# Attention row sums: half of the keys summed by ScalarE in PSUM, the other half as one chained slab

## The reference

```
h   = gamma * layernorm(x) + beta            # gamma, beta from the condition vector
qkv = h @ Wqkv.T + bqkv                       # split into q, k, v of 16 heads, 32 channels each
att = softmax(q @ k.T) / sqrt(512)            # per head, 1024 x 1024
out = (att @ v) @ Wp.T + bp
h1  = out + x
y   = gamma * layernorm(h1) + beta + h1
```

## Time and profile before

| | us |
|---|---|
| median of three runs (lowest, highest) | 1467.18 (1466.33, 1473.64) |
| the profiled execution | 1469.42 |
| its span, first to last instruction | 1467.8 |
| PE busy in the span | 1376.5 (94%) |
| POOL busy | 1004.2 (68%) |
| DVE busy | 918.7 (63%) |
| ACT busy | 708.4 (48%) |

### The profile page before, as it was taken

The page is one execution under the profiler, slowest core; times in us unless marked ns, Lnnn a source line. Parts: engine busy times, 40 slices in busy tenths (PEclk is TensorE's granted clock), DMA queues, the critical chain, the costliest instruction groups (busy, mean ns, idle before and its releaser), DMA issues.

```text
span 1467.8 us, 35271 instructions
## 1 busy us (share of the span) xinstructions
PE 1376.5 (94%) x10884; PEld 906.9 (62%) x10884; DVE 918.7 (63%) x1634; ACT 708.4 (48%) x1371; POOL 1004.2 (68%) x763
## 2 busy tenths in 40 slices
PE   6898999999999999999999999999999989898994
PEld 4888666656565767666666767666555545544562
DVE  5345766666666666666666666666666666666525
ACT  4121455555555545555454545555454545454441
POOL 2443455656565778688786978776898777778935
PEclk9899999999999999999999999999999999999997
DMA  7567533333434444455354444435453323332221
GB/s 232 149 185 224 130 97 100 100 98 102 114 101 115 118 121 137 117 139 141 108 144 122 135 110 136 116 113 141 116 134 85 103 85 102 86 101 87 76 60 61
DMA packets 216697, 174.01 MB, mean 119 GB/s; under 512 B 105492, under 2 KB 186516, under 8 KB 216632
## 3 DMA queue, kind: packets, MB, share of 16 engines
q1 hardware_dynamic: 214456, 166.83, 42.4%
q0 software_dynamic: 1984, 6.29, 1.2%
q10 hardware_dynamic: 192, 0.07, 0.0%
HBM read 113.29 MB, written 58.51 MB: 117 GB/s over the span
## 4 chain that ended last, share of the span: by engine, by line
PE 60%; POOL 18%; issue 12%; POOLq 3%; DVE 3%; DMA 1%; ACT 1%; SPq 1%; DVEq 0%; ACTq 0%
PE ps_a L744 12%; PE ps_st L758 10%; PE ps_o L775 10%; POOL p L1509 9%; PE ps_w L709 7%; PE ps_w L656 7%; PE ps_s L788 6%; PE ps_st L709 3%; POOLq L1369 2%; DVE half_max L1237 1%; POOL y_t L1426 1%; POOL y_t L1424 1%; PE ps_w L822 1%; POOL oT_s L1400 1%; PE ps_s L709 1%
## 5 line engine op out<-in xcount | busy, mean ns | idle before, releaser
L1237 DVE TENSOR_REDUCE half_max<-ps_a 128x1 f32<-128x512 f32 x1024 | 670.1, 687 | 404.1 <-PE ps_a L744 403.6
L1013 ACT ACTIVATE p<-ps_st 128x512 f32<-128x512 f32 x1024 | 565.9, 597 | 458.8 <-PE ps_st L758 427.5
L1509 POOL TENSOR_TENSOR p<-p 128x1024 f32<-128x1024 f32 x248 | 591.0, 2386 | 265.9 <-PE ps_o L775 264.3
L744 PE MATMUL ps_a<-k_stack,q_stack 96*128 96x512 f32 x1024 | 449.7, 441 | 14.7 <-DVE half_max L1237 10.7
L758 PE MATMUL ps_st<-q_stack,k_stack 98*128 98x512 f32 x1024 | 409.8, 402 | 15.2 <-ACT p L1013 14.6
L744 PEld LDWEIGHTS ps_a<-k_stack,q_stack 96*128 96x128 f32 x1024 | 194.0, 190 | 186.3 <-issue 94.8
L775 PE MATMUL ps_o<-p,v_head 128*32 128x256 f32 x4096 | 273.4, 385 | 0.0
L758 PEld LDWEIGHTS ps_st<-q_stack,k_stack 98*128 98x128 f32 x1024 | 196.4, 192 | 49.2 <-ACT p L1013 28.2
L775 PEld LDWEIGHTS ps_o<-p,v_head 128*32 128x32 f32 x4096 | 134.5, 111 | 91.3 <-issue 5.3
L788 PE MATMUL ps_s<-p,root_s 128*32 128x256 f32 x1984 | 160.5, 395 | 11.1 <-POOL p L1509 9.7
L709 PEld LDWEIGHTS ps_w<-hT_s,wqkv_s 128*128 128x128 f32 x1056 | 144.3, 189 | 11.0
(11 more groups left out here) (167 smaller groups left out, 1004.3 us busy)
## 6 DMA issues: line engine op xcount, KB each, us to landing
qk_scratch<-qkT_s SPq DMA_DIRECT2D x108, 256.0 KB, 2.4
q_stack<-qk_scratch SPq DMA_DIRECT2D x192, 128.0 KB, 2.8
k_stack<-qk_scratch SPq DMA_DIRECT2D x192, 128.0 KB, 3.0
x_tile<-in_x SPq DMA_DIRECT2D x34, 256.0 KB, 5.0
gq_s<-gain_bias_scratch SPq DMA_DIRECT2D x16, 512.0 KB, 4.4
v_scratch<-v_parts SPq DMA_DIRECT2D x32, 256.0 KB, 3.3
v_head<-v_scratch SPq DMA_DIRECT2D x64, 128.0 KB, 2.1
att_scratch<-o_stage SPq DMA_DIRECT2D x240, 32.0 KB, 1.5
```

Source lines behind the costliest of these rows:

```text
L744: pe.matmul(ps_a[:, parity, :], q_stack[0:96, s, t * 128:(t + 1) * 128], k_stack[0:96, s, half * 512:(half + 1) * 512], start=True, stop=T ...
L1013: nc.scalar.activation(p32[:, k, e * 512:(e + 1) * 512], ps_st[:, ST_BANK[2 * k + e], :], ACT.Exp).then_inc(exp_done, 1)
L1237: V.tensor_reduce(half_max[:, s % 2, item:item + 1], ps_a[:, parity, :], AX.X, ALU.max).then_inc(a_used, 1)
L1509: G.tensor_tensor(p32[:, 2 * j + 1, :], p32[:, 2 * j, :], p32[:, 2 * j + 1, :], ALU.add).then_inc(pair_added, 1)
```

## The change

Row sums are made in another way, and the maxima with them:

- A slab's two score matmuls (queries on partitions) now go to two neighbouring banks of a three-bank `ps_a`: the keys 512 to 1023 into bank 0 or 2 in turn (the kept bank), the keys 0 to 511 always into bank 1 (the shared bank). One DVE reduction over both banks (1024 columns) gives the negated maximum at once. `half_max` and its join are gone.
- ACT then takes the exponential of the kept bank in place, with `neg_max` as bias and an accumulator, which gives each query's sum over half of the keys (`slab_sum`, into `col_sums`). That is one more ACT operation of 512 columns in each step, beside the two it has.
- The other half of the keys is slabs 0 to 3 of the turned exponentials. POOL adds 0 to 1, that to 2, that to 3: three chained adds instead of four separate ones (`slab_add`).
- PE's row sums come once a head, in step 1 of the next (`row_sums`): 16 matmuls of 128 columns, 8 with `root_s` on slab 3 and 8 that turn `col_sums` with a scaled identity. They go into the free half of `ps_o`; `ps_s` is gone, its bank went to `ps_a`.
- ACT copies all 512 columns of `ps_o` in one instruction and waits for the row sums too. In the last iteration DVE's `end_norm` reads that copy.
- The turn of the maxima into a row uses the shared bank, after the slab of step 4. The start of the program puts 12 slabs where it had 25 items, and its projections use other banks.

The core of the diff:

```diff
-PAIR_ADD_STEP = {0: 2, 2: 3, 4: 0, 6: 1}
+SLAB_ADD_STEP = {4: 0, 6: 1, 7: 2}
...
-        ps_a = ctx.enter_context(nc.psum_tensor("ps_a", [128, 2, 512], F32))
+        ps_a = ctx.enter_context(nc.psum_tensor("ps_a", [128, 3, 512], F32))
         ps_o = ctx.enter_context(nc.psum_tensor("ps_o", [128, 512], F32))
-        ps_s = ctx.enter_context(nc.psum_tensor("ps_s", [128, 512], F32))
...
+        def slab_banks(t):
+            return (0, 1) if t % 2 == 0 else (2, 1)
...
+            def a_half(g, s, t, half, slab, uses):
+
+                kept, shared = slab_banks(t)
+                if half:
+                    need(pe, a_summed, slab - 1)
...
+                else:
+                    need(pe, a_used, uses)
+                mm = pe.matmul(ps_a[:, kept if half else shared, :], q_stack[0:96, s, t * 128:(t + 1) * 128],
+                               k_stack[0:96, s, half * 512:(half + 1) * 512], start=True, stop=True)
...
+            def turn(s, uses):
+
+                pe.wait_ge(a_used, uses)
+                pe.transpose(ps_a[0:8, 1, 0:128], neg_max[:, s % 2, :], f_ident).then_inc(a_ready, 1)
...
-            def pair_sums(g, s, j):
+            def row_sums(g, s):
...
+                pe.wait_ge(slab_added, 3 * v + 3)
+                pe.wait_ge(a_summed, 8 * v + 8)
+                for h in range(2):
+                    cols = slice(QW + h * 128, QW + h * 128 + 128)
+                    for e in range(4):
+                        pe.matmul(ps_o[HD * e:HD * e + HD, cols], root_s[:], p32[:, 3, e * QW + h * 128:e * QW + h * 128 + 128],
+                                  start=True, stop=False)
+                    for e in range(4):
+                        mm = pe.matmul(ps_o[HD * e:HD * e + HD, cols], col_sums[:, s, 2 * e + h:2 * e + h + 1].to_broadcast([128, HD]),
+                                       root_ident[:], start=False, stop=True)
...
                 act.wait_ge(pv_done, 4 * v + 4)
+                act.wait_ge(sum_done, v + 1)
...
+            def slab_sum(s, t, uses):
+
+                kept = slab_banks(t)[0]
+                act.wait_ge(a_used, uses)
+                nc.scalar.activation(ps_a[:, kept, :], ps_a[:, kept, :], ACT.Exp, bias=neg_max[:, s % 2, t:t + 1],
+                                     accum_out=col_sums[:, s, t:t + 1]).then_inc(a_summed, 1)
...
+            def slab_max(s, t, uses):
+
+                dve.wait_ge(a_ready, uses + 1)
+                low = min(slab_banks(t))
+                V.tensor_reduce(neg_max[:, s % 2, t:t + 1], ps_a[:, low:low + 2, :].rearrange("p a n -> p (a n)"), AX.X, ALU.max,
+                                negate=True).then_inc(a_used, 1)
...
+            def slab_add(g, s, j):
+
+                if j < 2:
+                    pool.wait_ge(pv_done, 16 * g + 4 * s + j + 1)
+                if j > 0:
+                    pool.wait_ge(slab_added, 12 * g + 3 * s + j)
+                G.tensor_tensor(p32[:, j + 1, :], p32[:, j, :], p32[:, j + 1, :], ALU.add).then_inc(slab_added, 1)
```

More of the change, by code:

```diff
@@ L834, in _ @@
             for step in range(LEAD_STEPS):
[L835 to L837 removed]
+                for use in LEAD_USES.get(step, ()):
+                    if use == "turn":
+                        turn(0, LEAD_TURN)
+                    else:
+                        for half in (1, 0):
+                            a_half(0, use // 8, use % 8, half, use, lead_count(use))
                 if step in LEAD_STAGE:
@@ L904, in iteration @@
                                     weighted(*before, j + 8)
+                            if k == 1 and behind:
+                                row_sums(*before)
                         project("end")
-                        if not last:
-                            for use in uses[2:]:
-                                a_item(*use)
+                        if not last and k == 4:
+                            turn((s + 1) % 4, uses + 1)
                         project("last")
```

254 lines of the change are left out of this document (98 added, 156 removed).

## The result

| | before | after |
|---|---|---|
| median of 4 runs, us | 1467.39 (1466.33 to 1473.64) | 1501.42 (1499.14 to 1503.85) |
| after / before | | 1.0223, 95% interval 1.019 to 1.0256 |
| span of the profiled execution, us | 1467.8 | 1497.5 |
| granted clock over the span | 0.977 | 0.968 |

The kernel became 2.2% slower. I had forecast 1465 us, no change. The time lies outside the forecast's own range (1452 to 1478); only the wide range of 1438 to 1508, which I had stretched over parts of the rivals, holds it.

What follows compares the result with a forecast made beforehand. PE's own stream was taken to bound full heads, DVE first and PE after light pairs. Terms -58 + 25 + 8 + 22 + 14 + 3 - 12 - 4 = -2 us, from 1467.18 to 1465 us; range 1452 to 1478, wide 1438 to 1508.

Steps and rivals of the forecast that it cites:

- What leaves and comes on PE, -58: PE's stream: old row sums and the last heads' line leave (122 us), new row-sum waves come (64 us).
- The turn, +25: Step 4 of some 42 full heads: the turn of the maxima waits 0.6 us more for the shared bank.
- Projections and late evacuations, +8: Full heads: 0.1 us a head where a projection stands between score matmuls, plus 3 us for few late evacuations.
- Light pairs and their turns, +22 and +14: Light heads: shared matmul 0.4 us later in 54 pairs of steps; with the turn, 0.75 in 18 heads.
- Start, +3, and tail, -4: Start: 12 slabs in a row held by the bank's chain, +3 us; last iteration: one POOL add less ahead, -4.
- POOL, -12: Light heads with output norms: fewer adds end sooner, taking back 12 us of PE's and ACT's waits for POOL.
- ACT, nothing: 512 more exponentials at 0.65 us each stay hidden, cost nothing while an operation stays under 0.75 us.
- Rival 2: ACT becomes the bound in light pairs through the accumulator's price: 1515 us, or 1485 at 0.85 a piece; chance 0.14.
- Rival 1: PE's gain stays because waits at turns and shared matmuls overlap: 1427 to 1450 us, say 1440; chance 0.25.
- Rival 3: The clock falls after PE's longer waits in light heads with the turn: +35 us, 1500; chance 0.12.
- Rival 4: Short row-sum waves cost as much as long ones, because weights bound them: -58 becomes -4, 1519 us; chance 0.07.

Runs made afterwards that it cites:

- experiment 4: Changed kernel with DVE's maximum taken over the shared bank's 512 keys alone, not both banks: 1418.52 us, 0.9658 of the kernel before.
- experiment 7: Changed kernel with the output norm's statistics over 32 columns instead of 512: 1497.55 us, 1.0181 of the kernel before.
- experiment 5: Changed kernel with ACT's new exponential (`slab_sum`) over 64 of its 512 columns: 1498.6 us, 1.0211 of the kernel before.
- experiment 12: Kernel before the change, with every second maximum over 64 of its 512 columns: 1459.65 us, 0.9933 of the unedited kernel.
- experiment 10: Changed kernel, maximum over the kept bank alone, shared score matmul left out, projection's first half behind the score matmuls: 1347.86 us, 0.9173 of the kernel before.
- experiment 9: Changed kernel, maximum over the shared bank alone, projection's first half moved behind the step's second score matmul: 1416.06 us, 0.964 of the kernel before.

## Why the prediction was wrong

Read step by step against its own sum:

- **What leaves and comes on PE, -58. A second step that failed, in light heads.** Right in size where PE sets the time: the sums take 0.99 us a head (1.0 forecast), and with the chain shortened a full head is 0.87 below before (0.84). Light heads gave less than I charged: iterations 11 to 14 of experiment 4 are 16 us below before, where 0.84 a head and POOL's 12 make 25, and the third light head there is only 0.3 below. I had charged light pairs as if the burst that left were worth all its length, though I had written that DVE sets them first.
- **The turn, +25.** Right: 0.53 us in place of 0.6.
- **Projections and late evacuations, +8. This is the step that failed.** I took the next shared matmul to follow "by some 1.75" behind a chain of 1.72. Left to itself it follows by 1.64, which could have been read off the kernel before. So there was no slack, and each place costs the 0.07 us that are missing and 0.10 more behind a matmul that was held: 0.17 us in steps 3 and 7 and 0.1 in step 1, 0.44 a head for the 0.1 I gave, some 14 us more in 42 heads. The late evacuations, put at 3 us in all, are 0.65 us in the last step of each iteration (3.35 against 2.70) and 2.0 us in step 1 of each light opening head (5.66 against 3.64): what DVE does between two slabs can now stand in PE's path (1.45 of those 2.0 us went when its statistics were cut short, experiment 7), where before the second bank took it up.
- **Light pairs and their turns, +22 and +14.** Right in a light head without norm work: turns there stood 16.6 us apart before, 17.7 after, 17.8 forecast. (In full heads I forecast 19.3 and they stand 19.8 to 20.0 apart, since even steps were 2.46 and not 2.35 already before; the sum goes by differences and doesn't feel it.) Heads with norm work or at the crossing of iterations cost more (+2.3 in the third head), for the reason just given.
- **Start, +3, and tail, -4.** Start, last iteration and end came to -4.3, where the same terms give -3.4.
- **POOL, -12.** The waits for its adds went as I said (18.0 and 20.8 us before; after, about 1 at the row sums and none at the exponentials). Steps 5 and 7 of the light opening heads fell from 8.4 to 6.9 us, 6 in all, half of the 12; step 1 of the same heads grew by 3.0 us, 2.0 of it by the chain (5.66 against 3.64 in experiment 4).
- **ACT, nothing.** Right, although an operation with its accumulator read is 0.87 us long by its rows, above my 0.75: the next one starts 0.68 us behind it, and relieving it gave 3 us (experiment 5). Rival 2 is out.
- **Rival 1** (waits overlap) is out: they added up. **Rival 3** (the clock) is real and small: the clock of iterations 11 to 14 fell from 0.98 to 0.94, for 8 us at most where I had 35. **Rival 4** (short waves cost as much) is out.

In sum: the chain cost up to 83 us where I had 72, and the rest gave at most 49 where I had 74. Where the line between the two lies is open by 11 us (experiment 4). So the savings, charged too high in light heads and at POOL, weigh at least as much as the waits charged too low; the 14 us in full heads stand in either case, since experiment 12 moved nothing there. Both errors come from one habit: I priced the chain step by step from the steady head, with slack read off as if it were spare, and priced the savings as if they lay everywhere on PE's path. "The Trainium skill", page "Perfetto Trace Analysis", section Matmuls, advises to rotate independent groups through different banks. This case's runs agree: half a microsecond of reduction a slab is worth 11 us with two banks in turn (experiment 12) and 83 us with one that every slab needs (experiment 4). I had weighed it only as a comment on the waits.

## What to carry to other kernels

When a change replaces two rotating banks by one that every step needs, its price isn't the wait in a steady step: add up everything that the engine freeing the bank does between two slabs, at the crossings of loops above all, and compare the chain's length with the least distance at which the other engine asks for the bank, to a tenth of a microsecond. An engine that is 58% busy and waits 470 us for PE can still set PE's time. A wait that is covered by reordering comes back at the next use of the same buffer, so shorten the chain: ask first whether the operation in it must read all that it reads; here a maximum over half the keys took 5.5% off the changed kernel, and leaving out the matmul that fed the other half took 5% more (experiment 10 against 9).

## What the runs showed of the hardware

- ACT's exponential with an accumulator is two instructions: 668 ns for 512 columns out of and into PSUM, and a read of the accumulator of 204 ns. The accumulator read does not push the next exponential by its whole length: the median distance from `slab_sum` to ACT's next start is 0.68 us.
- A reduction over 1024 columns across two banks takes 1224 ns, over one bank 691, over 2 columns of SBUF 155; the second 512 columns cost 533 ns, so no penalty for crossing the banks shows.
- A wave of four 128 x 32 weights and 128 columns each takes 0.11 us on PE (two are 0.22 us apart), with the weight loads in the shadow; eight of them with the step to the next matmul take 0.99.
- A score matmul that waits for its bank costs more than the wait: the next matmul starts 0.34 us behind it and not 0.23 (medians of the same 80 places, after and before).
- Half the clock (0.50 in a window) followed stretches in which PE was busy 1.79 of 3.40 us, and 0.63 of 3.30 us. With idle steps filled by repeated matmuls iterations 11 to 14 had a clock of 1.00 in place of 0.94.
